# A last stage in another order: GpSimd's row chain first, ScalarE's z in front of the scaling

## Chip, cores and metric

The kernel runs on one core of a Trainium2 chip (five engines: TensorE or PE, VectorE or DVE, ScalarE or ACT, GpSimd or POOL, and SyncE or SP, which issues transfers). The metric is the device time of one execution in microseconds.

## The reference

x is 64 batches of 128 tokens with 256 features. Four blocks follow one another, each with a layer norm in front and a gate tanh(g) on its result: cross attention with 16 heads, a mixture of 8 experts with one expert per token and a capacity, a second cross attention, and a dense mixture of 4 experts of which each token takes the best two. The change lies in the last block:

```python
def expert(w1, bb1, gg1, bbe1, w2, bb2, gg2, bbe2):
    h = jax.nn.relu(_layernorm(xf @ w1 + bb1, gg1, bbe1))
    return _layernorm(h @ w2 + bb2, gg2, bbe2)
gate_scores = xf @ gate_W + gate_b
topk_scores, topk_idx = jax.lax.top_k(gate_scores, 2)
weights = jax.nn.softmax(topk_scores, axis=-1)
all_out = jax.vmap(expert)(W1, b1, g1, be1, W2, b2, g2, be2)
out = sum over the two chosen of weights * all_out, plus xf
x = x + tanh(g_ffn[1]) * out          # xf = layernorm(x)
```

So each token needs three sets of row factors 1/sqrt(variance + 1e-5): one for xf, four for the first product of the experts (called h in the kernel), four for the second (called k).

## The kernel before

The work runs in phases: attention of the first layer, the eight experts, attention of the second layer, and the last stage, about 600 us at the end, which the function `fstep` writes out once for each engine. Its unit is a batch of 128 tokens, one on each partition. A step s of the loop holds pieces of several batches, a software pipeline by hand: each engine has its own list of pieces, in an order fixed by the text, and semaphores tie them together (`f["name"]`; a wait on `f["name"].at(b)` is a wait until the piece of batch b is done). Steps -4 to 2 are issued inside the end of the attention loop, 3 to 67 in a loop of their own; there are 64 batches.

What a batch b goes through, with the lines:

- VectorE takes its statistics `fmv` (L1379, L1383) in step b-2, adds the epsilon to the variance (L1385) and negates the mean (L1386). GpSimd makes `frs` in step b-1: power -0.5 (L622), times the negated mean (L624). ScalarE makes the normalised `xf` (L765). TensorE turns it (L1016), ScalarE copies the high part `xft_hi` (L770), VectorE takes the low part (L1368).
- In step b TensorE makes the first products of all four experts (L984) and the gates (L996, L998); VectorE takes `h_mv` (L1296, L1303) and adds the epsilon (L1305); GpSimd makes the factors `h_rs` with a power (L637); ScalarE scales the products into `z` (L785, `z1`), four operations; TensorE turns them (L1044); ScalarE applies gain, bias and relu (`a_t`, L805), eight operations. VectorE finds the best two gates (L1341 to L1364), ScalarE takes their exponential (`gexp`, L790), and VectorE makes the weights of the mixture in step b+1 (L1323 to L1330), which GpSimd adds up (`gw8`, L630).
- In step b+1 TensorE makes the bias (L1008) and the second products (L1025); VectorE takes `k_mv` (L1296, L1303, epsilon L1305) and multiplies the products by the gain out of PSUM into `u2g` (L1312).
- In step b+2 GpSimd makes `k_rs` with a power (L612) and `k_rw`, its product with the weights (L615); ScalarE scales `u2g` by it, four operations (L777); GpSimd adds them up: `u2s` (L643), `u2t` (L647), and with x `rest` (L649). TensorE turns the weights (L1035), ScalarE copies them (`gw_t`, L796).
- In step b+3 TensorE multiplies them by the last bias (L973), VectorE makes `mixed` (L1347), GpSimd makes the result `x4` (L656), and SyncE stores it (L504). SyncE loads `x3` four steps ahead (L500).

In step s GpSimd's list is: k_rs and k_rw (s-2), frs (s+1), gw (s-1), h_rs (s), u2s, u2t and rest (s-2), x4 (s-3). ScalarE's is: xf and xft_hi (s+1), the scaling of u2g (s-2), z (s), gexp (s), gw_t (s-2), a_t (s). TensorE's is L973 (s-3), L984 and the gates (s), L1008 (s-1), L1016 (s+1), L1025 (s-1), L1035 (s-2), L1044 (s). VectorE's is the weights (s-1), h_mv (s), the gates, mixed (s-3), the best two, xft_lo (s+1), the first half of k (s-1), fmv (s+2), the second half of k and k_mv (s-1).

Of the kernel before, what the change touches and what calls it, by code (L numbers as in the profile page):

```python
# [5 lines left out]
P = 128  # L6
ALU = mybir.AluOpType
ACT = mybir.ActivationFunctionType
# [104 lines left out]
def flamingo_gated(nc, x, ctx_in, consts, gates, wq, wk, wv, wp, b_proj, router, w1_0, b1_0, w2_0, b2_0,  # L113
                   gate_w, gate_w_first, w1_1, w1_first_1, b2_1, g1_1, be1_1, w2_1, g2_1, be2_1, out):
    B, S, D = x.shape
# [31 lines left out]
    with es:  # L147
# [234 lines left out]
        def signals(prefix, arrivals, counts):  # L382
# [33 lines left out]

        f = signals(
            "f_", {},
            dict(st=4, rstd=2, xf_done=1, x_turned=1, x_hi_done=1, x_lo_done=1, gates_done=1, gates_half=1, gates_read=1, gate_steps=4,
                 gexp_done=1, gate_mix=5, gwt_done=1, gw_turned=1, gw_t_done=1, up1_done=2, h_stats=9, h_rstd=1, z_act=4,  # L420
                 z_turned=2, a_done=8, down1_done=2, k_stats=9, k_rstd=2, u_done=2, u_scaled=4, be_done=1, mixed_done=1, halved=1,
                 summed=2, mix=1))
        f.update({name: arrival("f_" + name, ring=ring) for name, ring in dict(x3_came=8, x4_stored=2).items()})
        s_fw = sem("s_fw")
# [171 lines left out]
        def _(pool):  # L596
# [6 lines left out]
            pool.wait_ge(s_vz, 1)  # L603
            pool.memset(v_aug[:, :, :, DH:DH + 1], 1.0).then_inc(s_set, 1)
            def fstep(s):
                b = s - 2
                if b.within(B):
                    st = f["k_rstd"]
                    pool.wait_ge(f["k_stats"].of(b), f["k_stats"].at(b))
                    if (b - 1).begun:  # L610
                        pool.wait_ge(f["u_scaled"].of(b - 1), f["u_scaled"].at(b - 1))
                    nc.gpsimd.tensor_tensor(k_rs[:, 1, :], k_mv[:, :, 1], neg_half.to_broadcast([P, E1]), ALU.pow).then_inc(st.sem, 1)  # L612
                    pool.wait_ge(f["gwt_done"].of(b), f["gwt_done"].at(b))
                    pool.wait_ge(st.of(b), st.at(b, 1))
                    nc.gpsimd.tensor_tensor(k_rw[:], k_rs[:, 1, :], gw8[:, b.parity, 0:E1], ALU.mult).then_inc(st.sem, 1)  # L615
                b = s + 1
                if b.within(B):
                    st = f["rstd"]
                    pool.wait_ge(f["st"].of(b), f["st"].at(b))
                    if (b - 1).begun:  # L620
                        pool.wait_ge(f["xf_done"].of(b - 1), f["xf_done"].at(b - 1))
                    nc.gpsimd.tensor_tensor(frs[:, 1:2], fmv[:, 1:2], neg_half, ALU.pow).then_inc(st.sem, 1)  # L622
                    pool.wait_ge(st.of(b), st.at(b, 1))
                    nc.gpsimd.tensor_tensor(frs[:, 3:4], fmv[:, 0:1], frs[:, 1:2], ALU.mult).then_inc(st.sem, 1)  # L624
                b = s - 1
                if b.within(B):
                    pool.wait_ge(f["gate_mix"].of(b), f["gate_mix"].at(b))
                    if (b - 2).begun:
                        pool.wait_ge(f["gw_turned"].of(b - 2), f["gw_turned"].at(b - 2))
                    nc.gpsimd.tensor_tensor(gw8[:, b.parity, 0:E1], gwa[:], gwb[:], ALU.add).then_inc(f["gwt_done"].sem, 1)  # L630
                b = s
                if b.within(B):
                    st = f["h_rstd"]
                    pool.wait_ge(f["h_stats"].of(b), f["h_stats"].at(b))
                    if (b - 1).begun:
                        pool.wait_ge(f["z_act"].of(b - 1), f["z_act"].at(b - 1))
                    nc.gpsimd.tensor_tensor(h_rs[:, 1, :], h_mv[:, :, 1], neg_half.to_broadcast([P, E1]), ALU.pow).then_inc(st.sem, 1)  # L637
                b = s - 2
                if b.within(B):
                    pool.wait_ge(f["u_scaled"].of(b), f["u_scaled"].at(b))  # L640
                    if (b - 1).begun:
                        pool.wait_ge(f["summed"].of(b - 1), f["summed"].at(b - 1))
                    nc.gpsimd.tensor_tensor(u2s[:], u2g[:, b.parity, 0:2, :], u2g[:, b.parity, 2:4, :], ALU.add).then_inc(f["halved"].sem, 1)  # L643
                b = s - 2
                if b.within(B):
                    pool.wait_ge(f["halved"].of(b), f["halved"].at(b))
                    nc.gpsimd.tensor_tensor(u2t[:], u2s[:, 0, :], u2s[:, 1, :], ALU.add).then_inc(f["summed"].sem, 1)  # L647
                    pool.wait_ge(f["summed"].of(b), f["summed"].at(b, 1))
                    nc.gpsimd.tensor_tensor(rest[:, b.parity, :], u2t[:], x3[:, b.off % 8, :], ALU.add).then_inc(f["summed"].sem, 1)  # L649
                b = s - 3  # L650
                if b.within(B):
                    pool.wait_ge(f["summed"].of(b), f["summed"].at(b))
                    pool.wait_ge(f["mixed_done"].of(b), f["mixed_done"].at(b))
                    if (b - 2).begun:
                        pool.wait_ge(f["x4_stored"].of(b - 2), f["x4_stored"].at(b - 2))
                    nc.gpsimd.tensor_tensor(x4[:, b.parity, :], rest[:, b.parity, :], mixed[:, b.parity, :], ALU.add).then_inc(f["mix"].sem, 1)  # L656
# [96 lines left out]
        def _(act):  # L753
# [5 lines left out]
            def fstep(s):  # L759
                b = s + 1  # L760
                if b.within(B):
# [6 lines left out]
                    if (b - 2).begun:  # L768
                        act.wait_ge(f["gates_done"].of(b - 2), f["gates_done"].at(b - 2))
                    nc.scalar.activation(xft_hi[:, b.parity].rearrange("p c k -> p (c k)"), ps[:, 0, 0:D], ACT.Copy)\  # L770
                        .then_inc(f["x_hi_done"].sem, 1)
                b = s - 2
                if b.within(B):
                    act.wait_ge(f["u_done"].of(b), f["u_done"].at(b))
                    act.wait_ge(f["k_rstd"].of(b), f["k_rstd"].at(b))
                    for e in range(E1):
                        nc.scalar.activation(u2g[:, b.parity, e, :], u2g[:, b.parity, e, :], ACT.Copy, scale=k_rw[:, e:e + 1])\  # L777
                            .then_inc(f["u_scaled"].sem, 1)
                b = s
                if b.within(B):  # L780
                    act.wait_ge(f["h_rstd"].of(b), f["h_rstd"].at(b))
                    if (b - 2).begun:
                        act.wait_ge(f["z_turned"].of(b - 2), f["z_turned"].at(b - 2))
                    for e in range(E1):
                        nc.scalar.activation(z1[:, b.parity, e, :], ps[:, 2 + e // 2, (e % 2) * D:(e % 2 + 1) * D], ACT.Copy,  # L785
                                             scale=h_rs[:, 1, e:e + 1]).then_inc(f["z_act"].sem, 1)
                    act.wait_ge(f["gate_steps"].of(b), f["gate_steps"].at(b))
                    if (b - 1).begun:
                        act.wait_ge(f["gate_mix"].of(b - 1), f["gate_mix"].at(b - 1))
                    nc.scalar.activation(gexp[:], gdiff[:], ACT.Exp).then_inc(f["gexp_done"].sem, 1)  # L790
                b = s - 2
                if b.within(B):
                    act.wait_ge(f["gw_turned"].of(b), f["gw_turned"].at(b))
# [485 lines left out]
        def _(dve):  # L1279
# [18 lines left out]
            def stats_in_all(st, mv, sig, b):  # L1298
                dve.wait_ge(sig.of(b), sig.at(b, E1))
                if not b.known:  # L1300
                    carrier()
                for e in range(E1):
                    nc.vector.bn_aggr(mv[:, e, :], st[:, e, :]).then_inc(sig.sem, 1)  # L1303
                dve.wait_ge(sig.of(b), sig.at(b, 2 * E1))
                nc.vector.tensor_scalar(mv[:, :, 1], mv[:, :, 1], eps, None, ALU.add).then_inc(sig.sem, 1)  # L1305

            def out_of_psum(b, half):

# [6 lines left out]
            def fstep(s):  # L1315
# [16 lines left out]
                if b.within(B):  # L1332
                    stats(2, h_st, f["h_stats"], f["up1_done"], b, 0)
                    stats(2, h_st, f["h_stats"], f["up1_done"], b, 1)
                    if (b - 1).begun:
                        dve.wait_ge(f["h_rstd"].of(b - 1), f["h_rstd"].at(b - 1))
                    stats_in_all(h_st, h_mv, f["h_stats"], b)
                    dve.wait_ge(f["gates_done"].of(b), f["gates_done"].at(b))
                    nc.vector.tensor_copy(gpart[:], ps[:, 1, 128 + E1:128 + 2 * E1]).then_inc(f["gates_half"].sem, 1)
                    dve.wait_ge(f["gates_half"].of(b), f["gates_half"].at(b))  # L1340
                    nc.vector.tensor_tensor(gpad[:, b.parity, 0:E1], ps[:, 1, 128:128 + E1], gpart[:], ALU.add).then_inc(f["gates_read"].sem, 1)  # L1341
# [33 lines left out]
                if b.within(B):  # L1375
# [5 lines left out]
                    if not b.known:  # L1381
                        carrier()
                    nc.vector.bn_aggr(fmv[:], fst[:]).then_inc(f["st"].sem, 1)  # L1383
                    dve.wait_ge(f["st"].of(b), f["st"].at(b, 2))
                    nc.vector.tensor_scalar(fmv[:, 1:2], fmv[:, 1:2], eps, None, ALU.add).then_inc(f["st"].sem, 1)  # L1385
                    nc.vector.tensor_scalar(fmv[:, 0:1], fmv[:, 0:1], -1.0, None, ALU.mult).then_inc(f["st"].sem, 1)  # L1386
                b = s - 1
                if b.within(B):
                    stats(6, k_st, f["k_stats"], f["down1_done"], b, 1)
# [407 lines left out]
```

## Time and profile before

| | before |
|---|---|
| median of 3 runs | 2152.01 us |
| lowest, highest | 2150.12, 2153.9 us |
| the profiled execution | 2150.5 us |
| its span | 2148.7 us |
| mean granted clock of TensorE | 0.985 of full speed |
| busy in the span: PE, DVE, ACT, POOL | 96%, 82%, 70%, 57% |

A row of the order in time shows the start in us from the span's start, the time of the group, engine, line, operation, what it writes and reads, and how many instructions; in brackets how long the engine stood idle before and what ended that. The ends of matmuls are modelled. A start lies up to 0.1 us before the end of the instruction in front of it where an engine overlaps the two.

### The profile page before, as it was taken

The page shows a single profiled execution, that of the slowest core. Times are in us where ns is not written, and L with a number is a line of the kernel's source. Part 1 is how long each engine was busy: PE and PEld are TensorE (multiplying, and loading weights), DVE is VectorE, ACT ScalarE, POOL GpSimd, SP SyncE. Part 2 cuts the span into 40 slices and gives each one's busy share as a digit, 9 for nine tenths or more (in the row PEclk, how much of TensorE's full clock was granted, in tenths as well). Part 3 has the DMA queues.
Part 4 walks back from the last instruction along what each step waited for, and adds up shares of the span by engine and source line. Part 5 has one row for each costly group of instructions (what it writes and reads, how often), then busy time and mean ns, then how long its engine had stood idle before and what let it go on. Part 6 is the DMA issues. An engine that isn't in the chain of part 4 may idle for free.

```text
span 2148.7 us, 57822 instructions
## 1 busy us (share of the span) xinstructions
PE 2052.7 (96%) x19788; PEld 1790.2 (83%) x19788; DVE 1762.3 (82%) x4916; ACT 1501.9 (70%) x3234; POOL 1220.5 (57%) x1800
## 2 busy tenths in 40 slices
PE   6999999999699999999699999999899999999997
PEld 5888888888599999999588888888788888888885
DVE  5888888888588888888677777777599999999996
ACT  4766666666487877878366666666577787777785
POOL 5787878887300000000487878777367777777776
PEclk9999999999799999999899999999999999999998
DMA  6555221221466766665322222222101000000000
GB/s 230 188 180 166 64 68 61 70 63 54 158 240 225 248 222 246 223 244 212 135 68 76 72 73 70 71 76 65 41 23 31 31 28 27 30 30 30 30 25 18
DMA packets 151665, 226.12 MB, mean 105 GB/s; under 512 B 20454, under 2 KB 135786, under 8 KB 141036
## 3 DMA queue, kind: packets, MB, share of 16 engines
q1 hardware_dynamic: 145260, 205.99, 28.4%
q0 software_dynamic: 6144, 16.79, 2.6%
q8 instruction: 147, 2.41, 0.5%
q14 instruction: 114, 0.93, 0.1%
HBM read 153.77 MB, written 68.94 MB: 104 GB/s over the span
## 4 chain that ended last, share of the span: by engine, by line
PE 69%; DVE 12%; POOL 6%; issue 6%; DMA 3%; ACT 3%; POOLq 0%; SPq 0%; ACTq 0%; DVEq 0%
PE ps L1254 10%; PE ps L1270 10%; PE ps L1126 10%; PE ps L1111 5%; PE ps L1025 5%; PE ps L1065 4%; PE ps L1202 3%; PE ps L1214 3%; PE ps L1158 3%; DVE k_st L1296 2%; PE ps L984 2%; DMA slots_d<-rows,slot_s 2%; PE ps L1082 2%; POOL k_rs L612 2%; PE ps L1059 2%
## 5 line engine op out<-in xcount | busy, mean ns | idle before, releaser
L1406 DVE TENSOR_REDUCE nmax<-ps 128x16 f32<-128x2048 f32 x128 | 292.3, 2284 | 27.7 <-PE ps L1082 27.4
L873 ACT ACTIVATE prob_t<-ps 128x2048 f32<-128x2048 f32 x128 | 240.9, 1882 | 77.1 <-PE ps L1065 77.1
L688 POOL COPY slot_in<-slot_all 128x1 int32<-128x1 int32 x64 | 11.4, 178 | 472.9 <-DMA eo_d<-eo 472.9
L1025 PE MATMUL ps<-w2f,a_t 128*128 128x256 f32 x1024 | 231.7, 379 | 0.3 <-ACT a_t L805 0.3
L1254 PE MATMUL ps<-xgt_hi,w_hl 128*128 128x256 f32 x1248 | 229.9, 282 | 1.0 <-DVE xgt_lo L1671 1.0
L1270 PE MATMUL ps<-w_hl,hid_hi 128*128 128x256 f32 x1248 | 226.9, 284 | 0.0
L1025 PEld LDWEIGHTS ps<-w2f,a_t 128*128 128x128 f32 x1024 | 189.6, 190 | 23.8 <-ACT a_t L805 0.6
L662 POOL TENSOR_TENSOR km_r<-qk,cst 128x512 fp32r<-128x512 f32 x128 | 133.4, 1042 | 126.7 <-ACT qk L863 126.6
L945 ACT ACTIVATE hid<-ps,b_in 128x256 f32<-128x256 f32 x312 | 145.6, 468 | 82.9 <-PE ps L1254 67.4
L1254 PEld LDWEIGHTS ps<-xgt_hi,w_hl 128*128 128x128 f32 x1248 | 195.3, 189 | 1.4 <-issue 1.4
L805 ACT ACTIVATE a_t<-ps,be_in,g_in 128x128 f32<-128x128 f32 x512 | 185.5, 468 | 12.3 <-PE ps L1044 11.4
L1270 PEld LDWEIGHTS ps<-w_hl,hid_hi 128*128 128x128 f32 x1248 | 191.5, 188 | 0.0
L1662 DVE TENSOR_TENSOR w_hl<-w_raw,w_hl 128x1024 fp32r<-128x1024 f32 x152 | 176.0, 1219 | 15.3 <-ACT w_hl L921 15.3
L863 ACT ACTIVATE qk<-ps 128x512 f32<-128x512 f32 x128 | 76.5, 597 | 143.1 <-PE ps L1126 143.1
L1254 PE MATMUL ps<-xgt_lo,w_hl 128*128 128x256 f32 x624 | 176.3, 283 | 0.0
L1270 PE MATMUL ps<-w_hl,hid_lo 128*128 128x256 f32 x624 | 175.6, 281 | 0.0
L1687 DVE TENSOR_TENSOR hid_lo<-hid,hid_hi 128x256 fp32r<-128x256 f32 x312 | 132.6, 425 | 48.3 <-ACT hid_hi L951 42.6
L921 ACT ACTIVATE w_hl<-w_raw 128x1024 fp32r<-128x1024 f32 x152 | 148.2, 1058 | 0.0
L1126 PE MATMUL ps<-x_t,w_q 128*128 128x128 f32 x1024 | 145.7, 286 | 1.0 <-ACT x_t L827 0.9
L1111 PE MATMUL ps<-prob_t,v_aug 128*32 128x128 f32 x4096 | 138.5, 276 | 2.4 <-ACT v_aug L820 1.7
L1126 PEld LDWEIGHTS ps<-x_t,w_q 128*128 128x128 f32 x1024 | 127.0, 195 | 15.1 <-issue 12.7
L1126 PE MATMUL ps<-c_t,w_k 128*128 128x128 f32 x1024 | 138.6, 279 | 0.0
(230 smaller groups left out, 6270.8 us busy)
## 6 DMA issues: line engine op xcount, KB each, us to landing
w_raw<-in_w_dram SPq DMA_DIRECT2D x78, 1024.0 KB, 6.8
c_t<-in_ctx_in_dram SPq DMA_DIRECT2D x128, 128.0 KB
x_d<-x SPq DMA_DIRECT2D x128, 128.0 KB, 2.4
slots_d<-zeros SPq DMA_DIRECT2D x12, 1024.0 KB, 5.9
eo_d<-zeros SPq DMA_DIRECT2D x12, 1024.0 KB, 5.8
xg<-slots_d SPq DMA_DIRECT2D x39, 256.0 KB, 2.7
eo_d<-eo SPq DMA_DIRECT2D x39, 256.0 KB, 2.2
x_in<-in_x_dram SPq DMA_DIRECT2D x64, 128.0 KB, 2.2
```

The lines of the kernel that those rows point to most:

```text
L662: return nc.gpsimd.tensor_tensor(dst, src.unsqueeze(2).to_broadcast([P, 2, 2, P]), head_mask.unsqueeze(1).unsqueeze(3).to_broadcast([P, 2, ...
L805: nc.scalar.activation(a_t[:, b.parity, e, c, :], ps[:, 4 + e // 2, (e % 2 * 2 + c) * P:(e % 2 * 2 + c + 1) * P], ACT.Relu, scale=g1_in[:, ...
L873: nc.scalar.activation(prob_t[:].rearrange("p a k -> p (a k)"), scores.rearrange("p a k -> p (a k)"), ACT.Exp, scale=SOFT).then_inc(y["exp ...
L921: nc.scalar.activation(w_hl[:, g.parity, 0, cols], w_raws[g.parity][:, cols], ACT.Copy).then_inc(z["wh_done"].sem, 1)
L945: nc.scalar.activation(hid[:, fc % 4, :], ps[:, 2 + fc % 4, 0:G], ACT.Gelu, bias=b1_in[:, g.off % 3, fc:fc + 1]).then_inc(z["hid_done"].se ...
L1025: mm = pe.matmul(dst, a_t[:, b.parity, e, c, :], w2f[:, e, c, :], start=False, stop=True, skip_group_check=True)
L1111: mm = pe.matmul(b6[32 * g:32 * g + 32, j * P:(j + 1) * P], v_aug[:, p, h, :], prob_t[:, r, :], start=True, stop=True, tile_position=(0, 3 ...
L1126: mm = pe.matmul(b5[:, (part + m) * P:(part + m + 1) * P], w[:, c, m * P:(m + 1) * P], src[:, c, :], start=(c == 0), stop=(c == C - 1))
L1254: mm = pe.matmul(ps[:, 2 + fc % 4, 0:G], w_hl[:, q, w, at:at + P], xt[:, q, c, :], start=(k == 0), stop=(k == 5))
L1270: mm = pe.matmul(ps[:, q, i * D:(i + 1) * D], ht[:, fc, i * P:(i + 1) * P], w_hl[:, q, w, at:at + D], start=(fc == 0 and i == 0 and k == 0 ...
L1406: nc.vector.tensor_reduce(nmax[:, b.parity, :, 0:4], scores.rearrange("p a (r k) -> p a r k", k=P), AX_X, ALU.max, negate=True).then_inc(y ...
L1662: nc.vector.tensor_tensor(w_hl[:, g.parity, 1, cols], w_raws[g.parity][:, cols], w_hl[:, g.parity, 0, cols], ALU.subtract).then_inc(z["wl_ ...
```

## The change

GpSimd's frs chain moves to the head of its list, and it adds its own epsilons to the variances of xf and of k, and negates the product of mean and factor itself; VectorE's three small operations for that are gone (h keeps its own). On ScalarE the scaling of `u2g` moves from in front of `z` to behind `gexp`.

```diff
         f = signals(
-            dict(st=4, rstd=2, ... h_stats=9, ... k_stats=9, k_rstd=2, ...
+            dict(st=2, rstd=4, ... h_stats=9, ... k_stats=8, k_rstd=3, ...
 # GpSimd
             def fstep(s):
+                b = s + 1
+                if b.within(B):
+                    st = f["rstd"]
+                    pool.wait_ge(f["st"].of(b), f["st"].at(b))
+                    if (b - 1).begun:
+                        pool.wait_ge(f["xf_done"].of(b - 1), f["xf_done"].at(b - 1))
+                    nc.gpsimd.tensor_tensor(frs[:, 0:1], fmv[:, 1:2], eps, ALU.add).then_inc(st.sem, 1)
+                    pool.wait_ge(st.of(b), st.at(b, 1))
+                    nc.gpsimd.tensor_tensor(frs[:, 1:2], frs[:, 0:1], neg_half, ALU.pow).then_inc(st.sem, 1)
+                    pool.wait_ge(st.of(b), st.at(b, 2))
+                    nc.gpsimd.tensor_tensor(frs[:, 2:3], fmv[:, 0:1], frs[:, 1:2], ALU.mult).then_inc(st.sem, 1)
+                    pool.wait_ge(st.of(b), st.at(b, 3))
+                    nc.gpsimd.tensor_tensor(frs[:, 3:4], frs[:, 2:3], neg_one, ALU.mult).then_inc(st.sem, 1)
                 b = s - 2
                 if b.within(B):
                     st = f["k_rstd"]
...
-                    nc.gpsimd.tensor_tensor(k_rs[:, 1, :], k_mv[:, :, 1], neg_half.to_broadcast([P, E1]), ALU.pow).then_inc(st.sem, 1)
+                    nc.gpsimd.tensor_tensor(k_rs[:, 0, :], k_mv[:, :, 1], eps.to_broadcast([P, E1]), ALU.add).then_inc(st.sem, 1)
+                    pool.wait_ge(st.of(b), st.at(b, 1))
+                    nc.gpsimd.tensor_tensor(k_rs[:, 1, :], k_rs[:, 0, :], neg_half.to_broadcast([P, E1]), ALU.pow).then_inc(st.sem, 1)
...
-                b = s + 1
-                if b.within(B):
...
-                    nc.gpsimd.tensor_tensor(frs[:, 1:2], fmv[:, 1:2], neg_half, ALU.pow).then_inc(st.sem, 1)
-                    pool.wait_ge(st.of(b), st.at(b, 1))
-                    nc.gpsimd.tensor_tensor(frs[:, 3:4], fmv[:, 0:1], frs[:, 1:2], ALU.mult).then_inc(st.sem, 1)
 # ScalarE
-                b = s - 2
-                if b.within(B):
-                    act.wait_ge(f["u_done"].of(b), f["u_done"].at(b))
-                    act.wait_ge(f["k_rstd"].of(b), f["k_rstd"].at(b))
-                    for e in range(E1):
-                        nc.scalar.activation(u2g[:, b.parity, e, :], u2g[:, b.parity, e, :], ACT.Copy, scale=k_rw[:, e:e + 1])\
-                            .then_inc(f["u_scaled"].sem, 1)
                 b = s
...
                     nc.scalar.activation(gexp[:], gdiff[:], ACT.Exp).then_inc(f["gexp_done"].sem, 1)
+                b = s - 2
+                if b.within(B):
+                    act.wait_ge(f["u_done"].of(b), f["u_done"].at(b))
+                    act.wait_ge(f["k_rstd"].of(b), f["k_rstd"].at(b))
+                    for e in range(E1):
+                        nc.scalar.activation(u2g[:, b.parity, e, :], u2g[:, b.parity, e, :], ACT.Copy, scale=k_rw[:, e:e + 1])\
+                            .then_inc(f["u_scaled"].sem, 1)
 # VectorE: the epsilon in stats_in_all only for h now
-                    nc.vector.tensor_scalar(fmv[:, 1:2], fmv[:, 1:2], eps, None, ALU.add).then_inc(f["st"].sem, 1)
-                    nc.vector.tensor_scalar(fmv[:, 0:1], fmv[:, 0:1], -1.0, None, ALU.mult).then_inc(f["st"].sem, 1)
```

## Rows read from the trace of the kernel before

**Rows 1.** Busy time by stretch: stretch, its length, then PE, PEld, DVE, ACT, POOL, clock, DMA
```profile
1600.00:1700.00 100.00, 98.46 (x516) 81.80 (x514) 90.86 (x414) 79.63 (x220) 71.64 (x110) 1.00 0.10 30
...
1530.00:1540.00 10.00, 7.48 (x101) 6.02 (x94) 4.21 (x15) 5.59 (x10) 3.30 (x7) 1.00 0.23 66
```

**Rows 2.** Who waited for whom, 1560 to 2149 us: total us, times, longest
```profile
ACT xf L765 <- POOL frs L624: 68.8, 61, 1.5
POOL u2s L643 <- ACT u2g L777: 64.6, 63, 1.9
PEld ps L1016 <- ACT xf L765: 36.3, 61, 1.1
```

**Rows 3.** Order in time of GpSimd, one step of the last stage
```profile
2107.23 1.27 POOL L643 TENSOR_TENSOR u2s<-u2g 128x512 f32<-128x512 f32 x1 [0.90 <-ACT u2g L777]
2108.58 0.73 POOL L647 TENSOR_TENSOR u2t<-u2s 128x256 f32<-128x256 f32 x1
2109.39 0.73 POOL L649 TENSOR_TENSOR rest<-u2t,x 128x256 f32<-128x256 f32 x1
2110.07 0.74 POOL L656 TENSOR_TENSOR x<-rest,mixed 128x256 f32<-128x256 f32 x1
2111.01 1.01 POOL L612 TENSOR_TENSOR k_rs<-k_mv,cst 128x4 f32<-128x4 f32 x1 [0.20 <-DVE k_mv L1305]
2112.17 0.20 POOL L615 TENSOR_TENSOR k_rw<-k_rs,gw 128x4 f32<-128x4 f32 x1
2112.32 0.56 POOL L622 TENSOR_TENSOR frs<-fmv,cst 128x1 f32<-128x1 f32 x1
2112.95 0.19 POOL L624 TENSOR_TENSOR frs<-fmv,frs 128x1 f32<-128x1 f32 x1
2113.10 0.20 POOL L630 TENSOR_TENSOR gw<-gwa,gwb 128x4 f32<-128x4 f32 x1
2114.44 1.01 POOL L637 TENSOR_TENSOR h_rs<-h_mv,cst 128x4 f32<-128x4 f32 x1 [1.14 <-DVE h_mv L1305]
2116.36 1.27 POOL L643 TENSOR_TENSOR u2s<-u2g 128x512 f32<-128x512 f32 x1 [0.91 <-ACT u2g L777]
```

**Rows 4.** Order in time of ScalarE, the same step and the end of the one before
```profile
2107.05 1.55 ACT L785 ACTIVATE z<-ps,h_rs 128x256 f32<-128x256 f32 x4
2108.48 0.22 ACT L790 ACTIVATE gexp<-gdiff 128x1 f32<-128x1 f32 x1
2108.75 0.27 ACT L796 ACTIVATE gw_t<-ps 4x128 f32<-4x128 f32 x1
...
2113.18 0.60 ACT L765 ACTIVATE xf<-x,frs 128x256 f32<-128x256 f32 x1 [1.04 <-POOL frs L624]
...
2114.59 1.69 ACT L777 ACTIVATE u2g<-u2g,k_rw 128x256 f32<-128x256 f32 x4
2116.19 1.55 ACT L785 ACTIVATE z<-ps,h_rs 128x256 f32<-128x256 f32 x4
```

**Rows 5.** Order in time of GpSimd, h_rs of batches 3 and 63
```profile
1572.82 1.01 POOL L637 TENSOR_TENSOR h_rs<-h_mv,cst 128x4 f32<-128x4 f32 x1 [1.15 <-DVE h_mv L1305]
...
2123.59 1.01 POOL L637 TENSOR_TENSOR h_rs<-h_mv,cst 128x4 f32<-128x4 f32 x1 [2.04 <-DVE h_mv L1305]
```

**Rows 6.** Groups by shape of VectorE, 1560 to 2149 us: busy us, mean ns, idle before
```profile
L1305 DVE TENSOR_SCALAR k_mv<-k_mv,cst 128x4 f32<-128x4 f32 x64 | 15.3, 238 | 2.3
L1385 DVE TENSOR_SCALAR fmv<-fmv,cst 128x1 f32<-128x1 f32 x60 | 12.8, 214 | 2.1
L1386 DVE TENSOR_SCALAR fmv<-fmv 128x1 f32<-128x1 f32 x60 | 8.6, 143 | 0.0
```

**Rows 7.** Order in time of GpSimd in the first attention phase
```profile
499.87 0.18 POOL L669 TENSOR_TENSOR rs<-mv,cst 128x1 f32<-128x1 f32 x1
500.13 0.55 POOL L671 TENSOR_TENSOR rs<-rs,cst 128x1 f32<-128x1 f32 x1
```

**Rows 8.** Order in time of TensorE, the same step
```profile
2109.42 0.60 PE L973 MATMUL ps<-be_in,gw_t 128*128 128x256 f32 x2
```

More of the change, by code:

```diff
@@ L418, in flamingo_gated @@
             "f_", {},
-            dict(st=4, rstd=2, xf_done=1, x_turned=1, x_hi_done=1, x_lo_done=1, gates_done=1, gates_half=1, gates_read=1, gate_steps=4,
+            dict(st=2, rstd=4, xf_done=1, x_turned=1, x_hi_done=1, x_lo_done=1, gates_done=1, gates_half=1, gates_read=1, gate_steps=4,
                  gexp_done=1, gate_mix=5, gwt_done=1, gw_turned=1, gw_t_done=1, up1_done=2, h_stats=9, h_rstd=1, z_act=4,
-                 z_turned=2, a_done=8, down1_done=2, k_stats=9, k_rstd=2, u_done=2, u_scaled=4, be_done=1, mixed_done=1, halved=1,
+                 z_turned=2, a_done=8, down1_done=2, k_stats=8, k_rstd=3, u_done=2, u_scaled=4, be_done=1, mixed_done=1, halved=1,
                  summed=2, mix=1))
@@ L611, in fstep @@
                         pool.wait_ge(f["u_scaled"].of(b - 1), f["u_scaled"].at(b - 1))
-                    nc.gpsimd.tensor_tensor(k_rs[:, 1, :], k_mv[:, :, 1], neg_half.to_broadcast([P, E1]), ALU.pow).then_inc(st.sem, 1)
+                    nc.gpsimd.tensor_tensor(k_rs[:, 0, :], k_mv[:, :, 1], eps.to_broadcast([P, E1]), ALU.add).then_inc(st.sem, 1)
+                    pool.wait_ge(st.of(b), st.at(b, 1))
+                    nc.gpsimd.tensor_tensor(k_rs[:, 1, :], k_rs[:, 0, :], neg_half.to_broadcast([P, E1]), ALU.pow).then_inc(st.sem, 1)
                     pool.wait_ge(f["gwt_done"].of(b), f["gwt_done"].at(b))
-                    pool.wait_ge(st.of(b), st.at(b, 1))
+                    pool.wait_ge(st.of(b), st.at(b, 2))
                     nc.gpsimd.tensor_tensor(k_rw[:], k_rs[:, 1, :], gw8[:, b.parity, 0:E1], ALU.mult).then_inc(st.sem, 1)
-                b = s + 1
-                if b.within(B):
[L618 to L621, printed above, removed]
-                    nc.gpsimd.tensor_tensor(frs[:, 1:2], fmv[:, 1:2], neg_half, ALU.pow).then_inc(st.sem, 1)
-                    pool.wait_ge(st.of(b), st.at(b, 1))
-                    nc.gpsimd.tensor_tensor(frs[:, 3:4], fmv[:, 0:1], frs[:, 1:2], ALU.mult).then_inc(st.sem, 1)
                 b = s - 1
@@ L1303, in stats_in_all @@
                     nc.vector.bn_aggr(mv[:, e, :], st[:, e, :]).then_inc(sig.sem, 1)
-                dve.wait_ge(sig.of(b), sig.at(b, 2 * E1))
-                nc.vector.tensor_scalar(mv[:, :, 1], mv[:, :, 1], eps, None, ALU.add).then_inc(sig.sem, 1)
             def out_of_psum(b, half):
@@ L1337, in fstep @@
                     stats_in_all(h_st, h_mv, f["h_stats"], b)
+                    dve.wait_ge(f["h_stats"].of(b), f["h_stats"].at(b, 2 * E1))
+                    nc.vector.tensor_scalar(h_mv[:, :, 1], h_mv[:, :, 1], eps, None, ALU.add).then_inc(f["h_stats"].sem, 1)
                     dve.wait_ge(f["gates_done"].of(b), f["gates_done"].at(b))
@@ L1383, in fstep @@
                     nc.vector.bn_aggr(fmv[:], fst[:]).then_inc(f["st"].sem, 1)
-                    dve.wait_ge(f["st"].of(b), f["st"].at(b, 2))
-                    nc.vector.tensor_scalar(fmv[:, 1:2], fmv[:, 1:2], eps, None, ALU.add).then_inc(f["st"].sem, 1)
-                    nc.vector.tensor_scalar(fmv[:, 0:1], fmv[:, 0:1], -1.0, None, ALU.mult).then_inc(f["st"].sem, 1)
                 b = s - 1
```

## The prediction

> **What bounds the kernel now.** I read five views in this order: the busy times by stretch, who waited for whom, the order in time of GpSimd, then of ScalarE and of TensorE, and last the groups of instructions by shape.
>
> In the busy times of a stretch inside the last stage the reader sees TensorE at 98.46 of 100 us and VectorE at 90.86, with GpSimd at 71.64 [rows 1]. That would make TensorE the bound. But the waits of the stage [rows 2] say that ScalarE stood before `xf` for 68.8 us in 61 waits until GpSimd had its row factors `frs` (L624), and GpSimd stood before `u2s` for 64.6 us until ScalarE had scaled `u2g` (L777). Two engines that wait for each other once in every step form a loop, and the step can be no shorter than the loop.
>
> The loop is to be seen in one step of GpSimd and of ScalarE [rows 3, 4]. GpSimd: k_rs 2111.01, k_rw, frs (power) 2112.32, frs (product) 2112.95. ScalarE: xf 2113.18, then, behind the transposes, xft_hi and u2g at 2114.59, finished 1.69 us later. GpSimd: u2s 2116.36, u2t, rest, x4, and the next k_rs. One step lasts 9.13 us (u2s at 2107.23 and at 2116.36). Over the stage h_rs comes at 1572.82 for batch 3 [rows 5] and at 2114.44 for batch 62 [rows 3]: 541.6 us for 59 steps, 9.18 each. What matters below is that h_rs (L637) is outside of this loop: it ran from 2114.44 to 2115.45 while ScalarE scaled u2g.
>
> **The change part by part.** (1) Three small operations leave VectorE in each step: L1305 for k at 238 ns, L1385 at 214, L1386 at 143 [rows 6], some 0.6 us. VectorE isn't in the loop that I find below, so I count this as nothing; the cover is GpSimd's longer step, and if VectorE were the bound, it would be worth up to 0.6 us a step.
>
> (2) Three operations of the same size come to GpSimd: an addition in front of the frs power, a product by -1 behind it, an addition in front of the k power. In the attention phase such an addition took 0.18 us and the power that depends on it began 0.26 after it [rows 7]; with the 0.08 us from the end of one operation to a dependent one I take 0.27, 0.27 and 0.28. The lower bound is 0.15, the distance of two independent small ones (2112.95 and 2113.10 [rows 3]); the upper one 0.45, that distance and a small wait over. They can't give a gain by themselves, as they lie in GpSimd's order.
> The Trainium skill (GPSIMD Engine Reference, Engine selection) says that an elementwise operation with two inputs runs about twice as slowly on GpSimd as on VectorE. By that rule, twice the times on VectorE in part (1) are an estimate of 1.2 us a step instead of 0.8, and the sum below would end some 22 us higher; the row of the addition speaks against it.
>
> (3) GpSimd does the frs chain first. It needs only the statistics of the next batch, which VectorE has long before, so ScalarE's xf no longer waits for k_mv and k_rs. Alone this would open the present loop.
>
> (4) ScalarE makes z for batch s before it scales u2g for batch s-2. z waits for h_rs of batch s (GpSimd, L637); GpSimd's u2s, the next thing it does after h_rs, waits for all four scalings. Both engines take their instructions in the order of the program. So from now on h_rs, z, the exponential, the scaling and u2s stand one behind the other, and between h_rs and u2s GpSimd has nothing that it may do: u2t, rest, x4, the next frs chain, the next k chain, gw and the next h_rs are all queued behind u2s. The loop is all of GpSimd's step plus three things of ScalarE. From starts to starts in the rows:
> - h_rs 1.01 and 0.04 to the next engine: 1.05 (0.04 is what xf at 2113.18 waited after frs ended at 2113.14)
> - z to the exponential: 1.43 (2107.05 to 2108.48)
> - exponential to what follows it: 0.27 (2108.48 to 2108.75)
> - u2g to u2s: 1.77 (2114.59 to 2116.36)
> - u2s to u2t 1.35, to rest 0.81, to x4 0.68, and x4 to an operation that waits for nothing 0.69 (taken as from rest to x4): 3.53
> - frs: addition 0.27, power 0.63, product 0.27, sign to the next operation 0.15: 1.32
> - k: addition 0.28, power to k_rw 1.16 (2111.01 to 2112.17), k_rw to gw 0.15, gw to h_rs 0.15: 1.74
> All from [rows 3, 4] and part (2). Sum: 1.05 + 1.43 + 0.27 + 1.77 + 3.53 + 1.32 + 1.74 = 11.11 us, against 9.18: 1.93 us more in a step.
>
> Is the rest of the work ready for this loop? TensorE's weight loads stood 36.3 us in 61 waits before L1016 [rows 2], 0.6 each, a part of it beside the L1008 that still ran; I take 0.4, and its step is 9.13 less that, 8.7. The nearest other loop goes h_rs, z, exponential, u2g, gw_t (1.60 after u2g), L973 0.4 later, and from L973 to h_rs 5.02 (2109.42 to 2114.44 [rows 8, 3]): 1.05 + 1.43 + 0.27 + 1.60 + 0.4 + 5.02 = 9.77. It is shorter than 11.11 by 1.3 us, so h_mv will be ready before GpSimd comes to h_rs. Of the transfers, the load of x3 and the store of x4 are both on SyncE's queue and wait for GpSimd's rest and x4; both only come less often. Nothing is moved past a transfer on GpSimd's queue.
>
> (5) The ends of the stage. Between batches 3 and 62 there are 59 loops: 59 x 11.11 = 655.5 against 541.6, +113.9. The loop before them has no x4 yet and goes from 9.6 to about 10.4, +0.8; the one after them (batch 62 to 63, at 2123.59 [rows 5], 9.15 before) has no frs chain any more, 11.11 - 1.32 = 9.8, +0.6. In the tail the first u2s comes 1.05 + 1.43 + 0.27 + 1.77 = 4.5 after h_rs and not 1.0, as it does now right behind it: +3.5, and each of the two last k chains has 0.28 more, of which half lies beside waits of now: +0.4. Sum: +119.
>
> The profiled execution took 2150.5 us (span 2148.7), so its like becomes 2269.5; the median of the runs is 2152.0, 1.5 above it, and gives 2271.
>
> **The rivals.** *A: it is faster, TensorE's bound.* If the scaling were done early enough for GpSimd (say because z costs ScalarE nothing that GpSimd waits for), only part (3) would remain: the loop opens, TensorE no longer stands before L1016 and a step becomes 8.7: 60 x 0.45 = 27 us less, 2125. It decides from the point where h_rs to h_rs is below 9.1, that is if 2.0 us of my 11.1 weren't in series. For it: ScalarE waited 68.8 us for frs [rows 2]. Against it: for GpSimd to reach u2s early it would have to pass h_rs or ScalarE to pass z, and neither order allows it. 3%.
> *B: the nearest other loop decides.* If GpSimd's part were 1.3 us shorter than the rows say, the step is 9.77: 60 x 0.6 + 4 = 40 more, 2192. Nothing in the rows speaks for it. 3%.
> *C: TensorE's clock falls.* TensorE will be busy 8.7 of 11.1 us, with a stand of about 1.3 us before L1016. In a stretch where it was busy 7.48 of 10 us the granted clock was still 1.00 of 2.4 GHz [rows 1]. At 1.2 GHz, the other level, a step of TensorE would be at most 2 x 8.7 = 17.4 us, that is 59 x (17.4 - 9.18) = 485 more, 2637, and something between where only a part of the steps falls. The row with 7.48 speaks against it. 5%, the partial cases with it.
> *D: the change does nothing* (within 0.2%), as a gain from (3) and the loss of (4) cancel: they would have to be equal within 0.07 us a step. 1%.
>
> **How the numbers follow.** The forecast, 11.1 us a step, has 88%. The range: three additions at 0.15 instead of 0.27 make the step 0.37 shorter, 59 x 0.37 = 22, 2249; at 0.45 it is 0.53 longer, 31, 2302, but not all three at once are likely to be at the far end, so I take 2250 to 2295. Left out are A to D, 12%, and a little of the forecast's own. A measurement of this kernel tells about 0.2% from no change. Faster by over 0.2%: A, 3%. Within 0.2%: 1%. Slower: 96%.
>
> **What the profile after would show.** GpSimd's wait before u2s for u2g grows from 1.0 to about 3.5 us in each of some 60 steps, over 200 us in all, and is its only large wait: those before h_rs and k_rs are gone. h_rs comes every 11.1 us. z begins 0.04 us after h_rs ends and shows POOL h_rs as its releaser. xf begins right behind the frs chain, still waiting for GpSimd. TensorE's busy share of the last stage falls to about 80% and VectorE's to about 70%, at a clock of 1.00. I am wrong if u2s doesn't wait for ScalarE's scaling behind z, if h_rs waits for h_mv in most steps (B), or if the step is below 10.8 or above 11.6.

## The result and the profile after

The changed kernel takes 2262.99 us (median of 4, 2260.73 to 2263.88); the kernel before, on the same chip, 2151.07. The ratio is 1.0518, with an interval of 1.0499 to 1.0536: it is 112 us slower. The forecast was 2271, with a range of 2250 to 2295. The profiled execution has a span of 2262.1 us, 113.4 above that of before.

Where the time went, from the busy times by stretch of the changed kernel (stretch, length, PE, PEld, DVE, ACT, POOL, clock, DMA share, GB/s), to be read beside [rows 1]:

```profile
1600.00:1700.00 100.00, 84.69 (x433) 68.41 (x431) 76.17 (x320) 64.98 (x184) 63.08 (x117) 1.00 0.08 25
```

Every engine is busy less. Nothing has become a bound by its work, and TensorE's granted clock stayed at 1.00 in this stretch, though the engine stands 15 us in 100. So it is a wait, and the table of who waited for whom names it (total us, times, longest), beside [rows 2]:

```profile
POOL u2s L649 <- ACT u2g L795: 213.0, 64, 3.5
ACT xf L771 <- POOL frs L618: 131.3, 60, 2.3
...
ACT z L784 <- POOL h_rs L643: 74.3, 62, 3.6
...
POOL h_rs L643 <- DVE h_mv L1343: 1.7, 1, 1.7
```

GpSimd stood 213.0 us before u2s, 64.6 before the change. Its wait for h_mv, one of about 1.1 us a step before [rows 3], is gone: from batch 3 on GpSimd comes later than VectorE. And z, which never waited for h_rs in the steady part before, does so 62 times. Those are the two halves of one loop. The order in time of GpSimd, one step, beside [rows 3]:

```profile
1850.25 1.01 POOL L643 TENSOR_TENSOR h_rs<-h_mv,cst 128x4 f32<-128x4 f32 x1
1854.61 1.28 POOL L649 TENSOR_TENSOR u2s<-u2g 128x512 f32<-128x512 f32 x1 [3.35 <-ACT u2g L795]
...
1858.18 0.19 POOL L612 TENSOR_TENSOR frs<-fmv,cst 128x1 f32<-128x1 f32 x1
...
1859.50 0.20 POOL L625 TENSOR_TENSOR k_rs<-k_mv,cst 128x4 f32<-128x4 f32 x1
1859.78 1.01 POOL L627 TENSOR_TENSOR k_rs<-k_rs,cst 128x4 f32<-128x4 f32 x1
1860.87 0.20 POOL L630 TENSOR_TENSOR k_rw<-k_rs,gw 128x4 f32<-128x4 f32 x1
1861.02 0.20 POOL L636 TENSOR_TENSOR gw<-gwa,gwb 128x4 f32<-128x4 f32 x1
1861.19 1.01 POOL L643 TENSOR_TENSOR h_rs<-h_mv,cst 128x4 f32<-128x4 f32 x1
```

And what ScalarE does in the 3.35 us, beside [rows 4]:

```profile
1851.29 1.57 ACT L784 ACTIVATE z<-ps,h_rs 128x256 f32<-128x256 f32 x4 [1.15 <-POOL h_rs L643]
1852.73 0.22 ACT L789 ACTIVATE gexp<-gdiff 128x1 f32<-128x1 f32 x1
1852.83 1.71 ACT L795 ACTIVATE u2g<-u2g,k_rw 128x256 f32<-128x256 f32 x4
```

z starts 0.03 us after h_rs ends, the scaling 1.54 us after z started, and u2s 0.07 us after the scaling ended. From h_rs to h_rs it is 10.94 us, and this chain has no gap: while ScalarE makes z, the exponential and the scaling, GpSimd can only wait, and while GpSimd goes through its list, ScalarE can't begin the next z. What else ScalarE does (gw_t, a_t, xf, xft_hi) lies beside GpSimd's list. Over the stage batch 3 has its h_rs at 1575.30 and batch 62 at 2223.65, 648.35 us for 59 steps, 10.99 each, against 9.18.

### The profile page after: what moved, and what is told of

Same layout as the page of the kernel before. It is cut to its first block, busy times and chain, and to the rows that moved or that the text cites. A ratio compares the mean times of both kernels' runs of the same rounds, so it can differ in the third digit from the quotient of the medians.

```text
span 2262.1 us, 58032 instructions
## 1 busy us (share of the span) xinstructions
PE 2070.5 (92%) x19788; PEld 1793.7 (79%) x19788; DVE 1759.1 (78%) x4724; ACT 1490.4 (66%) x3234; POOL 1253.1 (55%) x1992
## 4 chain that ended last, share of the span: by engine, by line
PE 59%; POOL 18%; issue 8%; ACT 8%; DVE 4%; DMA 2%; POOLq 1%; ACTq 0%; SPq 0%; DVEq 0%
PE ps L1132 10%; PE ps L1260 10%; PE ps L1276 10%; PE ps L1117 5%; PE ps L1071 4%; POOL u2s L649 4%; ACT u2g L795 3%; ACT z L784 3%; PE ps L1208 3%; PE ps L1220 3%; POOL h_rs L643 3%; PE ps L1164 3%; POOL k_rs L627 3%; POOL u2t L653 2%; PE ps L1065 2%
## 5 line engine op out<-in xcount | busy, mean ns | idle before, releaser
L1031 PE MATMUL ps<-w2f,a_t 128*128 128x256 f32 x1024 | 231.7, 379 | 0.2 <-ACT a_t L811 0.2
L1031 PEld LDWEIGHTS ps<-w2f,a_t 128*128 128x128 f32 x1024 | 189.8, 190 | 23.7 <-ACT a_t L811 0.6
L649 POOL TENSOR_TENSOR u2s<-u2g 128x512 f32<-128x512 f32 x64 | 81.8, 1278 | 213.0 <-ACT u2g L795 213.0
L1302 DVE BATCH_NORM_STATS2 h_st<-ps 128x6 f32<-128x256 f32 x256 | 97.6, 423 | 90.8 <-PE ps L990 90.8
L784 ACT ACTIVATE z<-ps,h_rs 128x256 f32<-128x256 f32 x256 | 100.2, 474 | 76.9 <-POOL h_rs L643 76.9
```

The lines of the kernel that those rows point to most:

```text
L1031: mm = pe.matmul(dst, a_t[:, b.parity, e, c, :], w2f[:, e, c, :], start=False, stop=True, skip_group_check=True)
```

## The experiments

Each was timed next to the kernel before on the same chip. Four take the change apart.

**ScalarE's list put back, all else as changed.**

```diff
 # ScalarE, the changed kernel
+    scaling of u2g (s-2)      # L783: back in front of z
     z (s), gexp (s)
-    scaling of u2g (s-2)
     gw_t (s-2), a_t (s)
```

> The changed kernel with ScalarE's list put back: the scaling of u2g in front of z. GpSimd keeps the frs chain first and its own epsilons. Theory (the loss is the loop h_rs, z, scaling, u2s through GpSimd's whole list): the loop is open, GpSimd's own loop is 8.3 us and TensorE's 8.7 a step, so about 2125 us, faster than both kernels. Rival (the loss is GpSimd's longer chain and its additions): slower than 2151, near 2185.

2126.34 us, ratio 0.9885 (0.9869 to 0.9902). Not only is the loss gone, this is 25 us faster than the kernel before. What bounds it is TensorE's own work. Busy times by stretch, and the chain that ended last in order of time (start, us, what):

```profile
1600.00:1700.00 100.00, 100.00 (x535) 85.78 (x534) 88.20 (x398) 82.88 (x228) 80.50 (x151) 1.00 0.10 32
```

```profile
1850.52 3.46 PE ps L1031 x16
1853.97 0.11 PE ps L1041
1854.08 0.87 PE ps L1050 x8
1854.96 0.43 PE ps L979 x2
1855.39 2.80 PE ps L990 x12
...
1858.53 0.56 PE ps L1014 x2
1859.09 0.22 PE ps L1022 x2
1859.31 3.46 PE ps L1031 x16
```

The chain runs on TensorE alone, 8.79 us from L1031 to L1031. So the one edit on ScalarE costs 2263 - 2126 = 137 us in the company of the others.

**z first, alone.**

```diff
 # ScalarE, the kernel before
-    scaling of u2g (s-2)
     z (s), gexp (s)
+    scaling of u2g (s-2)
     gw_t (s-2), a_t (s)
```

> The kernel before with ScalarE's list alone changed: z in front of the scaling of u2g. GpSimd's list and VectorE's epsilons as before. Theory: the same loop without GpSimd's three additional operations, 10.2 us a step, about 2215 us. Rival (the loss is GpSimd's longer chain): 2151, unchanged.

2245.98 us, ratio 1.0435 (1.0418 to 1.0453). The edit alone makes it slower by 95 us, which the rival excluded, but it is 31 us above my number, 0.5 us a step. Its own rows show why. GpSimd:

```profile
1849.57 1.01 POOL L612 TENSOR_TENSOR k_rs<-k_mv,cst 128x4 f32<-128x4 f32 x1
1850.73 0.20 POOL L615 TENSOR_TENSOR k_rw<-k_rs,gw 128x4 f32<-128x4 f32 x1
1850.90 0.56 POOL L622 TENSOR_TENSOR frs<-fmv,cst 128x1 f32<-128x1 f32 x1
1851.54 0.22 POOL L624 TENSOR_TENSOR frs<-fmv,frs 128x1 f32<-128x1 f32 x1
1851.72 0.20 POOL L630 TENSOR_TENSOR gw<-gwa,gwb 128x4 f32<-128x4 f32 x1
1851.87 1.00 POOL L637 TENSOR_TENSOR h_rs<-h_mv,cst 128x4 f32<-128x4 f32 x1
1856.61 1.28 POOL L643 TENSOR_TENSOR u2s<-u2g 128x512 f32<-128x512 f32 x1 [3.73 <-ACT u2g L789]
...
1860.17 1.01 POOL L612 TENSOR_TENSOR k_rs<-k_mv,cst 128x4 f32<-128x4 f32 x1
```

ScalarE:

```profile
1851.80 0.60 ACT L765 ACTIVATE xf<-x,frs 128x256 f32<-128x256 f32 x1 [2.55 <-POOL frs L624]
1852.93 0.39 ACT L770 ACTIVATE xft_hi<-ps 128x256 fp32r<-128x256 f32 x1 [0.53 <-PE ps L1016]
1853.21 1.57 ACT L778 ACTIVATE z<-ps,h_rs 128x256 f32<-128x256 f32 x4
1854.63 0.23 ACT L783 ACTIVATE gexp<-gdiff 128x1 f32<-128x1 f32 x1
1854.73 1.72 ACT L789 ACTIVATE u2g<-u2g,k_rw 128x256 f32<-128x256 f32 x4
```

h_rs is ready at 1852.87, but z starts at 1853.21, with no wait for h_rs: it stands behind xf and xft_hi on ScalarE, and xf waits for frs, which here is still behind k_rs. The loop that decides isn't the one through h_rs, but k_rs, frs, xf, transposes, xft_hi, z, scaling, u2s. From starts to starts it is 1.33 to frs, 0.90 to xf, 1.41 to z, 1.42 to the exponential, 0.10 to the scaling, 1.88 to u2s and 3.56 to the next k_rs, 10.6 us, where I had summed only the loop through h_rs, 10.2.

That is not all of the 31 us. TensorE stands 1.4 to 1.7 us in front of L1016 in most steps of this kernel, and eight times between batches 3 and 62 its granted clock fell from 2.4 to 1.2 GHz (0.50) right behind such a stand, for under 4 us. One of them, by the busy times of a stretch (as above) and the rows of TensorE:

```profile
1755.50:1758.50 3.00, 3.00 (x9) 2.38 (x8) 0.75 (x2) 3.00 (x10) 0.00 (x0) 0.50 0.03 5
```

```profile
1754.64 0.44 PE L1016 MATMUL ps<-cst,xf 128*128 128x128 f32 x2 [1.58 <-ACT xf L765]
1754.92 5.30 PE L1025 MATMUL ps<-w2f,a_t 128*128 128x256 f32 x16
```

At the full clock L1025 takes 3.62 us. Behind it gw_t waited 1.73 us for TensorE and the next h_rs 1.25 us for h_mv. From h_rs to h_rs such a step is 12.02 us in the mean of the eight, the one after it 10.25, and the 43 undisturbed ones are 10.55. So 59 x (10.55 - 10.2) = 21 of the 31 us are the loop through xf, and 8 x (12.02 + 10.25 - 2 x 10.55) = 9 are the clock. All four executions of this kernel show a mean granted clock of 0.979 or 0.980, where all other kernels here show 0.983 or more.

**The epsilons and the sign on GpSimd, alone.**

```diff
 # GpSimd, the kernel before
     k_rs (s-2):  + addition of eps in front of the power
     frs (s+1):   + addition of eps in front, + product by -1 behind
 # VectorE
-    the addition of eps for k, that for fmv, the product by -1 for fmv
```

> The kernel before with the epsilons and the sign moved to GpSimd alone: both lists in the old order. Theory: the old loop k_rs, frs, xf, scaling, u2s, rest, x4 gets 0.28 and 0.27 and 0.27 us longer, less the 0.2 that GpSimd waited for VectorE's k_mv: 9.7 us a step, about 2186 us. Rival (VectorE is the bound, and relief of 0.6 us there pays): 2120 to 2151.

2183.58 us, ratio 1.015 (1.0133 to 1.0167), within 3 us of the sum. The three operations lie in the old loop as they lie in the new one, and no gain from VectorE's relief shows.

**frs first, alone.**

```diff
 # GpSimd, the kernel before
+    frs (s+1)
     k_rs, k_rw (s-2)
-    frs (s+1)
     gw (s-1), h_rs (s), ...
```

> The kernel before with GpSimd's frs chain moved to the head of its list alone: VectorE keeps its epsilons and the sign, ScalarE its list. Theory: the old loop is open; the next bounds are TensorE with 8.7 and VectorE with 8.8 us a step, so 2128 to 2133 us, a little above the same with GpSimd's epsilons. Rival (frs was hidden anyway): 2151.

2127.78 us, ratio 0.989 (0.9873 to 0.9906): 23 us faster, by moving one piece of one list. With the epsilons on GpSimd it was 2126.34, and the intervals overlap: VectorE was busy 93.72 us in 100 here and 88.20 there, and TensorE 100.00 in both. VectorE's 0.6 us a step don't show, nor do GpSimd's three operations: neither engine is in what bounds these two kernels.

Four more ask the changed kernel about its loop.

**h_rs in front of the k chain.**

```diff
 # GpSimd, the changed kernel
     frs (s+1)
+    h_rs (s)
     k_rs, k_rw (s-2), gw (s-1)
-    h_rs (s)
     u2s, u2t, rest (s-2), x4 (s-3)
```

> The changed kernel with one piece of GpSimd's list moved: h_rs in front of the k chain, so frs, h_rs, k_rs, k_rw, gw, u2s. The same operations, ScalarE's list as changed. Theory (between h_rs and u2s GpSimd can do nothing, and what is put there is free): k chain and gw fill the 3.35 us wait; the next loop is frs, xf, xft_hi, z, exponential, scaling, u2s, u2t, rest, x4: 1.39 + 1.13 + 0.28 + 1.43 + 0.10 + 1.78 + 3.57 = 9.7 us a step against 10.98, so about 2186 us. Rival (the number of operations on GpSimd decides): 2263, unchanged.

2204.02 us, ratio to the kernel before 1.0246 (1.0229 to 1.0263): with not one operation less, it is 59 us faster than the changed kernel. The wait before u2s is where the k chain went, for it fell to 109.9 us. It is 18 us above my sum: from h_rs of batch 3 to h_rs of batch 62 a step is 9.94 and not 9.7 us. Rows of two steps of GpSimd, and two of ScalarE:

```profile
1851.75 1.01 POOL L625 TENSOR_TENSOR h_rs<-h_mv,cst 128x4 f32<-128x4 f32 x1 [0.78 <-DVE h_mv L1343]
...
1856.11 1.28 POOL L649 TENSOR_TENSOR u2s<-u2g 128x512 f32<-128x512 f32 x1 [1.67 <-ACT u2g L795]
...
1861.52 1.01 POOL L625 TENSOR_TENSOR h_rs<-h_mv,cst 128x4 f32<-128x4 f32 x1 [0.49 <-DVE h_mv L1343]
...
1866.05 1.28 POOL L649 TENSOR_TENSOR u2s<-u2g 128x512 f32<-128x512 f32 x1 [1.79 <-ACT u2g L795]
```

```profile
1851.00 0.60 ACT L771 ACTIVATE xf<-x,frs 128x256 f32<-128x256 f32 x1 [1.69 <-POOL frs L618]
...
1862.65 1.57 ACT L784 ACTIVATE z<-ps,h_rs 128x256 f32<-128x256 f32 x4
```

h_rs waits for h_mv again. From xf at 1851.00 the work goes over L1022, L1031, L1050, L979 and L990 to h_mv and to h_rs at 1861.52, in the next step; from there over z and the scaling to u2s at 1866.05, and over frs (1869.62) to xf at 1871.08. That is a loop of 20.1 us over two steps in these rows, 19.9 in the mean, where I had only looked for loops of one step. It runs nearly level with the one that I had summed: z, at 1862.65, starts right behind xft_hi, which was done at 1862.66, and h_rs had been done at 1862.53. Over the stage steps of some 9.7 to 9.9 us, in most of which z starts right behind xft_hi as summed, alternate with steps of some 10.1, in which z comes later, behind h_rs. That this loop is the cause is read from the rows; no run was made against it.

**One more operation on GpSimd.**

```diff
 # GpSimd, the changed kernel, between gw and h_rs
+    nc.gpsimd.tensor_tensor(idle[:, 0:1], eps, neg_half, ALU.pow)
```

> The changed kernel with one more power of 128x1 on GpSimd in each step, between gw and h_rs, on constants, its result used by nothing. Theory (GpSimd's whole list is in the loop): 0.52 us more in each of some 61 steps, 2295 us. Rival (GpSimd stands 3.35 us in each step and has room): 2263.

2294.76 us, 32 more than the changed kernel, as summed from the loop. The added operation starts 0.52 us before h_rs, and the wait behind stays:

```profile
1864.64 0.55 POOL L642 TENSOR_TENSOR idle<-cst 128x1 f32<-128x1 f32 x1
1865.16 1.02 POOL L649 TENSOR_TENSOR h_rs<-h_mv,cst 128x4 f32<-128x4 f32 x1
1869.53 1.28 POOL L655 TENSOR_TENSOR u2s<-u2g 128x512 f32<-128x512 f32 x1 [3.35 <-ACT u2g L801]
```

An engine that is idle 3.35 us in each step has no room at all if the work is put in front of the operation that others need.

**More work on VectorE.**

```diff
 # VectorE, the changed kernel, in front of the statistics of h
+    for n_i in range(2):
+        nc.vector.bn_stats(idle[:, 6 * n_i:6 * n_i + 6], g2_in[:, 0, :])
```

> The changed kernel with two more statistics of 128x256 on VectorE in each step, in front of those of h, on constants, their result used by nothing: some 0.8 us. Theory (VectorE is outside of the loop, h_mv is ready 1.4 us before GpSimd comes to h_rs): no change, 2263 to 2266 us. Rival (VectorE is in the loop, and its relief of 0.6 us was worth something): 2295 to 2312.

2265.12 us, against 2262.99: within the spread of both (2261.5 to 2267.1, 2260.73 to 2263.88). 0.74 us a step on VectorE cost nothing. VectorE does the added work where it stood before the statistics of h for L990: that wait fell from 85.0 to 44.8 us.

**Both orders, VectorE's epsilons kept.**

```diff
 # GpSimd, the changed kernel
     frs (s+1):   - addition of eps, - product by -1
     k_rs (s-2):  - addition of eps
 # VectorE: its three operations are back
```

> The kernel before with both lists in the new order and VectorE keeping the epsilons and the sign: the changed kernel without GpSimd's three additional operations. Theory: 11.0 less 0.27, 0.27 and 0.27, so 10.2 us a step and about 2215 us; it would be below the 2246 of the kernel in which z was moved alone, since there frs came behind the k chain and z waited for xf. Rival (what moving z alone cost is a floor of this order of ScalarE): 2240 to 2263.

2216.06 us, ratio 1.03 (1.0283 to 1.0317). The three operations cost 47 us in the changed kernel, 0.78 us a step, where 0.82 were summed. And the two orders without them cost 65 us. Beside the kernel in which z alone was moved (2246) it is 30 us faster: with frs at the head z no longer stands behind xf, and the loop through h_rs is the longest again. Some 9 of the 30 us are the eight falls of the clock, of which this trace has none from 1560 to 2200 us: TensorE's stands are at most 0.7 us long here. So the frs chain at the head pays in either order of ScalarE, only less than z in front takes.

## Why the prediction was right

- **The loop.** The mechanism is as predicted: h_rs, z, exponential, scaling and u2s one behind another, with all of GpSimd's list behind them. Shown by the rows, by the change of ScalarE's list back (137 us), by the added operation on GpSimd that passed through in full, and by h_rs moved in front of the k chain.
- **Its length.** 11.11 us were summed, 10.94 came in the step shown and 10.99 in the mean. The term that was off is "exponential to what follows it: 0.27". What followed in [rows 4] was gw_t; the scaling, which follows now, starts 0.10 us after the exponential. The other terms came within 0.1: h_rs to z 1.04, z to the exponential 1.44, scaling to u2s 1.78, u2s to frs 3.57. 59 x (11.11 - 10.99) is 7 us too much. That the forecast ended 8 too high is in part luck: the first h_rs of the stage came 1.9 us later than before (1546.6 against 1544.7), which no term has, and against that the median was put 1.5 us above the profiled execution, while it came 0.9 below it.
- **The three operations.** 0.27, 0.27 and 0.28 were taken from one row of the attention phase. In the changed kernel the first power follows its addition by 0.26 and the k power by 0.28. The product by -1 took 189 ns where VectorE had needed 143, the additions 191 and 201 where it had needed 214 and 238 [rows 6]. The Trainium skill (GPSIMD Engine Reference, Engine selection) puts an elementwise operation with two inputs on GpSimd at about twice its time on VectorE. For these three, on tiles of 128x1 and 128x4, the rows don't agree: 1.3, 0.9 and 0.8 times (VectorE read one tile in each, GpSimd two).
- **VectorE's relief at nothing.** Right: +0.74 us there changes nothing, and in the faster version either place for the epsilons gives the same time.
- **The order of an engine's list.** GpSimd passed nothing in front of the blocked u2s, and ScalarE nothing in front of z. The Trainium skill (PSUM — Partial Sum Buffer, Engine vs sequencer instructions) has this as a rule: the queues of ScalarE, VectorE and GpSimd are "strict FIFO". The trace agrees: in the 3.35 us before u2s no row of GpSimd stands, and so in all 64 of these waits (213.0 us).
- **The ends.** The loop in front came with 10.28 us (10.4 predicted), the one behind with 9.68 (9.8), and the tail is 3.7 us longer (3.9).
- **The rivals.** A, TensorE as the bound, is just what comes when ScalarE's list is left alone, 2126 us for the 2125 of the text. B's loop isn't reached: h_mv was ready at 1859.78, 1.4 us before h_rs began at 1861.19 (1.3 predicted). C didn't come, the clock stayed at 1.00 from 1560 to 2230 us. But it was nearer than the row with 7.48 us of 10 let it seem: with z alone moved the clock fell eight times, at some 9 us in all, the partial case of C.
- **Small misses.** TensorE's and VectorE's shares were put at 80 and 70 in 100; they are 85 and 76. The two sums that missed by more were made after, for the experiments: once a second loop of one step was left out, and the falls of the clock, once a loop of two steps.

## What to carry to other kernels

Where two engines hand work to each other within a step, write down every loop from each of an engine's instructions back to itself, in the order of both lists and over two steps as well, before an order is changed: the step is the longest of them, whatever the busy shares say. An operation moved in front of another on one engine is also moved in front of everything that waits for that other, here GpSimd's whole list. In a list with a fixed wait, put the operation that starts the other engine as early as it may go and the rest behind it: that alone gave back 59 of 112 us here. To leave ScalarE's list as it was and move only frs to the head made the kernel 1.1% faster than it had been.

## What was not expected of the hardware

Additions and products of 128x1 and 128x4 take GpSimd 0.19 to 0.20 us, less than the 0.21 to 0.24 us of VectorE's additions of the same shapes. In the changed kernel TensorE stands up to 1.25 us at a stretch in the steady part and is busy 85 us in 100, and the granted clock was 1.00 of 2.4 GHz there, as it had been at 7.48 busy us of 10 [rows 1]. With one more operation on GpSimd it was busy only 80 to 81 in 100, in two stands of mostly about 1.1 us a step, still at 1.00. With z alone moved it was busy more, 85 to 88 in 100, but with one stand of mostly 1.4 to 1.7 us in a step, and the clock fell to 1.2 GHz eight times.
